# Layer 1's first three value copies: from DVE to ACT, their zero rows to POOL

## What is computed

```
qkv = jnp.einsum('bsd,od->bso', x, w_qkv)          # 32 query heads, 8 key and 8 value heads, 64 wide
q = _rms_norm(q, q_norm_w); k = _rms_norm(k, k_norm_w)
q, k = _rope(q, k, PAST_LENGTH)                    # q*cos + rot_half(q)*sin
scores = jnp.einsum('bhqd,bhkd->bhqk', q, k_rep) * scale + sliding_mask   # window of 64
probs = jax.nn.softmax(scores, axis=-1)
attn = jnp.einsum('bhqk,bhkd->bhqd', probs, v_rep)
out = jnp.einsum('bso,do->bsd', attn, w_out)
```

## Time and profile before

| | us |
|---|---|
| median of 3 runs | 514.9 |
| lowest and highest | 514.25, 515.71 |
| the profiled execution, whole time | 516.0 |
| its span, first to last instruction | 513.8 |

### The profile page before, as it was taken

The page is one execution under the profiler, slowest core; times in us unless marked ns, Lnnn a source line. Parts: engine busy times, 40 slices in busy tenths (PEclk is TensorE's granted clock), DMA queues, the critical chain, the costliest instruction groups (busy, mean ns, idle before and its releaser), DMA issues.

```text
span 513.8 us, 10828 instructions
## 1 busy us (share of the span) xinstructions
PE 475.2 (92%) x3858; PEld 398.9 (78%) x3858; DVE 385.1 (75%) x678; ACT 335.5 (65%) x942; POOL 239.9 (47%) x167
## 2 busy tenths in 40 slices
PE   6899988999999977999999999989999699999995
PEld 4454553878888966889999999877988588889884
DVE  4666488778543799998898988999998965554634
ACT  4656557544634349998888988878988799333230
POOL 0494637121623575755566575555548621320001
PEclk9999999999999989999999999999999899999998
DMA  7411000033401000000000000001001301100101
GB/s 273 158 42 43 2 1 1 5 120 92 124 25 38 1 1 1 22 22 4 20 23 22 22 23 22 2 22 41 23 3 50 114 5 60 42 1 0 42 0 41
DMA packets 8899, 19.96 MB, mean 39 GB/s; under 512 B 1424, under 2 KB 2960, under 8 KB 8720
## 3 DMA queue, kind: packets, MB, share of 16 engines
q1 hardware_dynamic: 8848, 19.29, 12.0%
HBM read 18.23 MB, written 1.05 MB: 38 GB/s over the span
## 4 chain that ended last, share of the span: by engine, by line
PE 74%; DVE 12%; ACT 6%; issue 4%; DMA 1%; POOL 1%; DVEq 0%; SPq 0%; POOLq 0%; ACTq 0%
PE psum L503 16%; PE psum L505 15%; PE psum L504 15%; PE psum L750 5%; PE psum L762 4%; PE psum L740 4%; PE psum L578 4%; PE psum L596 3%; PE psum L721 3%; ACT probs L1021 3%; PE psum L730 2%; DVE minus_max L1308 2%; DVE square_sums L1270 1%; DVE roped L1293 1%; DMA raw_chunks<-in_w 1%
## 5 line engine op out<-in xcount | busy, mean ns | idle before, releaser
L1021 ACT ACTIVATE probs<-psum,minus_max 128x128 f32<-128x128 f32 x256 | 91.6, 396 | 15.9 <-issue 7.8
L1428 POOL TENSOR_TENSOR rope_sin_part<-qkv_rows,sin_weighted 128x640 f32<-128x640 f32 x32 | 51.1, 1619 | 47.6 <-DVE rope_cos_part L1277 41.2
L1437 POOL TENSOR_TENSOR rms_inverse<-rms_inverse,minus_half 128x20 f32<-128x20 f32 x16 | 63.5, 3969 | 1.3
L1021 ACT ACTIVATION_READ_ACCUMULATOR probs<-psum,minus_max 128x1 f32 x256 | 60.1, 235 | 0.0
L989 ACT CAST hidden_high<-hidden 128x512 fp32r<-128x512 f32 x32 | 19.9, 620 | 61.2 <-DVE hidden L1223 61.2
L1308 DVE TENSOR_REDUCE minus_max<-psum 128x4 f32<-128x512 f32 x64 | 42.0, 684 | 16.2 <-PE psum L740 15.3
L503 PE MATMUL psum<-x_t_high,ug_high_low 128*128 128x512 f32 x128 | 51.2, 400 | 0.6 <-ACT silu_gate L987 0.6
L505 PE MATMUL psum<-x_t_high,ug_high_low 128*128 128x512 f32 x128 | 50.7, 396 | 0.0
L504 PE MATMUL psum<-x_t_low,ug_high_low 128*128 128x512 f32 x128 | 50.5, 395 | 0.0
L503 PE MATMUL psum<-qkv_high_low,x_t_high 128*128 128x384 f32 x128 | 46.7, 365 | 3.7 <-ACT qkv_rows L994 1.7
L1302 DVE TENSOR_TENSOR probs<-probs,prob_inverse 128x512 f32<-128x512 f32 x64 | 47.8, 747 | 2.2
(11 more groups left out here) (156 smaller groups left out, 1382.0 us busy)
## 6 DMA issues: line engine op xcount, KB each, us to landing
raw_chunks<-in_ug SPq DMA_DIRECT2D x8, 512.0 KB, 3.9
raw_chunks<-in_wout SPq DMA_DIRECT2D x16, 256.0 KB, 2.8
raw_chunks<-in_qkv SPq DMA_DIRECT2D x8, 384.0 KB, 3.3
down_tree<-in_down SPq DMA_DIRECT2D x1, 1024.0 KB, 8.2
x_rows<-in_x_rows SPq DMA_DIRECT2D x2, 512.0 KB, 5.1
raw_chunks<-in_down SPq DMA_DIRECT2D x2, 512.0 KB, 3.9
raw_chunks<-in_x SPq DMA_DIRECT2D x2, 256.0 KB, 3.5
raw_chunks<-in_w SPq DMA_DIRECT2D x2, 256.0 KB, 4.6
```

The source lines that it names most:

```text
L1021: e = nc.scalar.activation(pr[:, c, q, :], o[:, q * P:(q + 1) * P], ACT.Exp, bias=negm[:, c, q:q + 1], accum_out=psum1[:, c, q:q + 1])
L1428: last = nc.gpsimd.tensor_tensor(ov[:, :, :, z, :], rv[:, :, :, 1 - z, :], sv[:, :, :, z, :], ALU.mult)
L1437: nc.gpsimd.tensor_tensor(r, r, half[:], ALU.pow).then_inc(rr_done, 1)
```

## The change

In passes 0, 1 and 2 the three copies of values1 are issued by ACT, and the zero rows by POOL, ahead of sines(k). ACT gets a function values1 for it, and SCALAR_FILL three entries: values1(0) behind squares(0), values1(1) behind squares(1), values1(2) behind squares(2). VECTOR_FILL loses its first three. DVE's values1(3), the first that stays, waits until the three on ACT have counted, so that `v1_done` stays in order. Nothing is computed otherwise, and passes 3 to 15 are as before.

```diff
+VALUES_ON_ACT = 3
...
-    ("up", 0, 14), ("squares", 0), ("up", 0, 15), ("proj1", 1, 0), ("proj1", 1, 1), ("proj1", 1, 3), ("proj1", 1, 2),
+    ("up", 0, 14), ("squares", 0), ("values1", 0), ("up", 0, 15), ("proj1", 1, 0), ("proj1", 1, 1), ("proj1", 1, 3),
...
+            def values1(k):
+
+                slot, r = k % 5, qraw[:, k % 2]
+                for t in range(TT):
+                    emptied(act, ("proj1", k, t))
+                nc.scalar.copy(v1[:, slot, 0, :, :], r[:, :, GW:GV])
+                nc.scalar.copy(v1[0:64, slot, 1, 1:TT, :], r[64:128, 0:TT - 1, GW:GV])
+                nc.scalar.copy(v1[64:128, slot, 1, :, :], r[0:64, :, GW:GV]).then_inc(v1_done, 1)
...
+                if k == VALUES_ON_ACT:
+                    dve.wait_ge(v1_done, VALUES_ON_ACT)
...
             def sines(k):
+                if k < VALUES_ON_ACT:
+                    nc.gpsimd.memset(v1[0:HD1, k % 5, 1, 0, :], 0.0)
```

More of the change, by code:

```diff
@@ L155 @@
     ("chunk", ("qkv", 7)), ("proj1", 0, 1), ("proj1", 0, 0), ("up", 0, 13), ("proj1", 0, 3), ("proj1", 0, 2),
[5 rows of a table removed]
[L161 to L168, removed]
-    ("square_sums", 1), ("values1", 1), ("normed", 0), ("values1", 2), ("cosines", 1), ("xt", 2, 1),
-    ("square_sums", 2), ("rope_sums", 1), ("maxima", 0, 0), ("normed", 1), ("maxima", 0, 1), ("cosines", 2),
-    ("maxima", 0, 2), ("maxima", 0, 3), ("probs", 0, 1), ("values1", 3), ("probs", 0, 0), ("probs", 0, 3),
-    ("probs", 0, 2), ("rope_sums", 2), ("maxima", 1, 0), ("square_sums", 3), ("maxima", 1, 1), ("normed", 2),
-    ("maxima", 1, 2), ("maxima", 1, 3), ("pv1", 0, 0), ("cosines", 3), ("probs", 1, 1), ("probs", 1, 0),
-    ("pv1", 0, 1), ("probs", 1, 3), ("probs", 1, 2), ("values1", 4), ("rope_sums", 3), ("maxima", 2, 0),
-    ("maxima", 2, 1), ("square_sums", 4), ("normed", 3), ("maxima", 2, 2), ("maxima", 2, 3), ("pv1", 1, 0),
-    ("cosines", 4), ("probs", 2, 0), ("probs", 2, 1), ("pv1", 1, 1), ("probs", 2, 2)]
[5 rows of a table added]
@@ new lines @@
+    ("proj1", 4, 0), ("squares", 3), ("turn_p", 0, 2), ("turn_p", 0, 1), ("turn_p", 0, 0), ("exps", 1, 0),
+    ("proj1", 4, 2), ("exps", 1, 1), ("wout", 0), ("pv1", 0, 0), ("proj1", 4, 3), ("turn_p", 0, 3), ("exps", 1, 2),
+    ("exps", 1, 3), ("pv1", 0, 1), ("proj1", 5, 1), ("squares", 4), ("turn1q", 2, 1), ("turn_p", 1, 1), ("turn1k", 2),
+    ("turn1q", 2, 0), ("proj1", 5, 0), ("turn_p", 1, 0), ("turn_p", 1, 2), ("exps", 2, 0), ("exps", 2, 1),
+    ("turn_p", 1, 3), ("pv1", 1, 0), ("wout", 1), ("proj1", 5, 3), ("exps", 2, 2), ("exps", 2, 3), ("pv1", 1, 1),
@@ new lines @@
+    ("proj1", 5, 2)]
+VECTOR_FILL = [("up", 0, 10), ("up", 0, 11), ("up", 0, 12), ("xt", 2, 0), ("up", 0, 13), ("up", 0, 14), ("up", 0, 15),
+    ("square_sums", 0), ("cosines", 0), ("ln_add", 1, 1, 0), ("ln_stats", 1, 1, 0), ("ln_add", 1, 1, 1),
+    ("ln_stats", 1, 1, 1), ("rope_sums", 0), ("ln_norm", 1, 1, 0), ("ln_norm", 1, 1, 1), ("square_sums", 1),
+    ("normed", 0), ("cosines", 1), ("xt", 2, 1), ("square_sums", 2), ("rope_sums", 1), ("maxima", 0, 0),
+    ("normed", 1), ("maxima", 0, 1), ("cosines", 2), ("maxima", 0, 2), ("maxima", 0, 3), ("probs", 0, 1),
+    ("values1", 3), ("probs", 0, 0), ("probs", 0, 3), ("probs", 0, 2), ("rope_sums", 2), ("maxima", 1, 0),
+    ("square_sums", 3), ("maxima", 1, 1), ("normed", 2), ("maxima", 1, 2), ("maxima", 1, 3), ("pv1", 0, 0),
+    ("cosines", 3), ("probs", 1, 1), ("probs", 1, 0), ("pv1", 0, 1), ("probs", 1, 3), ("probs", 1, 2), ("values1", 4),
+    ("rope_sums", 3), ("maxima", 2, 0), ("maxima", 2, 1), ("square_sums", 4), ("normed", 3), ("maxima", 2, 2),
+    ("maxima", 2, 3), ("pv1", 1, 0), ("cosines", 4), ("probs", 2, 0), ("probs", 2, 1), ("pv1", 1, 1), ("probs", 2, 2)]
@@ L1045, in wout @@
                 chunk(("wout", k))
-            in_pass = dict(proj1=proj1, turn1k=turn1k, turn1q=turn1q, turn_p=turn_p, pv1=pv1, squares=squares,
+            in_pass = dict(values1=values1, proj1=proj1, turn1k=turn1k, turn1q=turn1q, turn_p=turn_p, pv1=pv1, squares=squares,
                             exps=exps, wout=wout)
```

## The result

The changed kernel took 518.82 us, median of 5 runs (515.71 to 519.75), and the kernel before 515.41 beside it (514.25 to 516.16). The ratio is 1.0067, with an interval of 1.0047 to 1.0087: slower by 0.67%, 3.4 us. I had forecast 515.2 us with a range up to 516.6. The profiled execution took 519.75 us with a span of 518.0, the longest of the five.

The account below looks back on a forecast made before the run. Where layer 1's attention starts, DVE's chain to maxima(0,0), tied with POOL's sines(1), was taken to set the pace, not TensorE. +0.25 (POOL) +0.02 (silu) +0 (k_t) = +0.3 us on 514.9 gave 515.2 us, range 513.8 to 516.6.

Parts of the forecast that it names:

- POOL gets in between two products: At normed(0)'s two DVE products: POOL's scaling, asked at 183.02, is held only until 183.54 and ends at 183.62.
- +0.25 for POOL: At rope_sums(1): sines(1) on POOL ends at 191.24 instead of 190.99, so rope_sums(1) starts 0.25 us later.
- The step that I had called the weakest: After square_sums(1): normed starts at 182.86, only 0.16 us ahead of POOL's request; if behind, the sign turns.
- cosines(1) is long over: At sines(1) on POOL: DVE's cosines(1) no longer holds it, so it takes 3.06 us instead of 4.18.
- The memset: On POOL ahead of sines(0), (1) and (2): each takes 0.11 us, at most 0.2.
- values1(1) on ACT: On ACT from about 179.95: the copies of proj1(2,...) behind it end within 0.05 us of before; cost 0.
- k_t: Copy on ACT: gains 0.98 us from the earlier normed(0), loses 0.97 to values1(2); start stays at 189.95, cost 0.
- The cover of 0.6 us: Between scores1(0,0) ending at 191.78 and DVE coming at 192.50: 0.6 us of cover, just used up by the upper bound.
- values1(0): On ACT ahead of the silu at 167.81: silu ends near 169.14, hidden waits till 169.22 anyway; cost 0.02, at most 0.7.
- rival 3: TensorE's clock falls behind the gap before k_t's copy: +0.7, up to +1.7 us; chance 0.14.
- +0.3: Whole forecast delay up to the first exponentials: +0.25 (POOL) +0.02 (silu) +0 (k_t, covered) = +0.3 us.

Follow-up runs that it names:

- e2: Kernel before with only values1(1) moved to ACT, its zero row to POOL; values1(0) and values1(2) stay on DVE: ratio 1.0032.
- e3: The change with one semaphore wait on DVE between normed(0)'s two products: ratio 1.0042.
- e12: Kernel before with only values1(2) moved to ACT, ahead of the copies of q and k: ratio 0.9995.
- e1: The change with values1(1) back on DVE, values1(0) and values1(2) still on ACT: ratio 1.0038.
- e5: The change with 7, 5 and 11 extra TensorE products that nobody reads, in three of its pauses: ratio 1.0042.
- e16: The change, unaltered, run and profiled a second time: ratio 1.0068, 517.84 us.
- e13: Kernel before with only values1(0) moved to ACT, its zero row to POOL: ratio 1.0014.
- e6: e1 with 7, 5 and 4 extra TensorE products that nobody reads, in three pauses: ratio 1.0003.
- e4: The change with 16 extra TensorE products that nobody reads, ahead of scores1(0,1): ratio 1.0064.
- e10: The change with e3's wait on DVE and 6, 5 and 4 extra TensorE products in its pauses: ratio 1.0003.
- e14: The change with values1(0) back on DVE, values1(1) and values1(2) still on ACT: ratio 1.0050.

## Why the prediction was wrong

**The step that failed** is "POOL gets in between two products". It rested on the earlier trace rows, where the power, begun inside a DVE product, ended 3.39 us behind it although the next product had started. I took that for a rule of any two products. But the program has DVE wait for semaphores ahead of its product at 244.32, satisfied by then (the row has no idle time), and none stands between normed(0)'s two products. After the change the scaling was held to the end of both, 1.71 us instead of my 0.60 (e2 repeats it, e3 with a wait between them gives 0.58). The error ran on: the power asked at 185.14, 3.36 us behind square_sums(1) instead of my 2.24, so it missed the time in which POOL was free and fell into cosines(1), 4.77 us instead of 4.37. My +0.25 for POOL was +1.7. The step that I had called the weakest held: normed(0) started 0.17 us ahead of POOL's request (183.18 and 183.35), where I had 0.16.

**What followed from it and was right.** sines(1) took 3.03 us, as "cosines(1) is long over" had it. The memset took 0.14, bound 0.11 to 0.2. The Trainium skill (SBUF — State Buffer, Who interferes with whom) says that a GpSimd instruction that only writes isn't concerned; the trace agrees, since the memset at 197.98 took 0.14 us inside cosines(2), and the sines behind it 3.77. That section also says that issue order decides who blocks. It doesn't say who is next when DVE has its next product ready while GpSimd waits, and that was the point here: POOL's scaling starts in the trace at 183.35, 0.42 us ahead of the second product at 183.77, and ends behind it.

**values1(1) on ACT** cost nothing, as said. **k_t** started at 190.05 (said: 189.95) and the scores at 190.69; they ended at 191.85, long before DVE came at 194.56, so this branch wasn't the last one. The cover of 0.6 us was never put to the test by the change. Without the gain of the earlier normed(0) it is just used up: in e12 and e1 DVE waits 0.49 us for the scores, and maxima(0,0) stands 0.06 us later than in the kernel before.

**values1(0)** was mis-sized. ACT of the kernel after:

```profile
167.55 0.39 ACT L1002 COPY v_rows<-qkv_rows 128x256 f32<-128x256 f32 x1
167.95 0.35 ACT L1003 COPY v_rows<-qkv_rows 64x192 f32<-64x192 f32 x1
168.31 0.40 ACT L1004 COPY v_rows<-qkv_rows 64x256 f32<-64x256 f32 x1
168.74 0.69 ACT L988 ACTIVATE silu_gate<-psum,scale_ug 128x512 f32<-128x512 f32 x1
```

The copies are a little shorter than my 0.43, 0.38 and 0.43, but they don't overlap with each other or the silu, though squares(0) ahead of them overlaps the first by 0.10 (166.38 + 1.27 against 167.55): 1.19 us from the first start to the silu's, not 0.97. hidden now waits for the silu and stands 4.46 us behind the one before it instead of 4.23: +0.23 us, where I had +0.02. The estimate from the Trainium skill (ScalarE: Activation LUTs, Rules for kernel authors) had been 1.21 and 0.26, nearer than my rows, and by luck: its 0.3 us and 0.83 ns an element, meant for an ACTIVATE with a pointer operand, give 0.51, 0.46 and 0.51 us for the three copies, and the overlap that I took off wasn't there.

**TensorE's clock** was rival 3. Its condition was "more than TensorE's pause of 1.04 us at 196.20", and the pause became 3.03. Its chance, 0.14, was too small; I had reckoned it with the +0.3 ahead of it, and not with +1.7. It is worth about 1.2 us on average (e5 against the change), within the 0.7 to 1.7 that I gave it, and that is partly luck, for the place and the length were wrong: in the first profile the fall that cost lay from 199.6 us on, lasted 6.8 us and not the 3.4 behind my 1.7, and cost 1.84 (59.64 against e16's 57.80); in e16 it lay where I had put it, and there it cost next to nothing.

**The sum, as measured**: hidden +0.23, POOL +1.7, and 0.27 us that both profiles of the change show between square_sums(5) and square_sums(12) give 2.2 us, which is e5's 0.42% and the difference of the spans in its profile (516.0 and 513.8). The clock's 1.2 makes it 3.4. I had +0.25, +0.02 and nothing.

**What stays open.** Which pause brings the clock down in e1 isn't settled: its parts e12 and e13 measured 0.9995 and 1.0014, and together they made 1.0038. That it is the clock rests on e6 and on the missing long executions there. Why the clock falls now here, now there in executions of one kernel no run shows. The cause of the 0.27 us behind square_sums(5) is open as well. In the change it lies between square_sums(8) and square_sums(9), 15.39 us instead of 15.13, and all profiles with three values1 on ACT have it (e3, e4, e5, e10, e16). With two of them (e1, e6, e14) 0.13 us stand between square_sums(5) and square_sums(12), with one none. And why a DVE wait that is long satisfied lets POOL in as the unsatisfied one of e3 does isn't shown.

## What to carry to other kernels

Before taking short one-input work off DVE, look at what stands on both sides of it and whether POOL is waiting then: copies between two-input products can be the only time in which POOL gets through. Where such products must stand back to back, a semaphore wait between them, 0.13 us here, lets POOL in and brought the first maxima 1.4 us forward. And a change of TensorE's pauses can cost more than the delay on the path: here some 2.2 us of delay came with about another 1.2 through the clock, and in e3 0.3 us at the first maxima came with 2.0.
